# Moebius rounds: products of up to four tiles in one instruction, their sums in another, three buffers

## The reference, cut to what matters

```python
def mobius_add(x, y):
    x2 = jnp.sum(x * x, axis=-1, keepdims=True)
    y2 = jnp.sum(y * y, axis=-1, keepdims=True)
    xy = jnp.sum(x * y, axis=-1, keepdims=True)
    num = (1.0 + 2.0 * xy + y2) * x + (1.0 - x2) * y
    den = 1.0 + 2.0 * xy + x2 * y2
    return num / jnp.maximum(den, EPS)
...
messages = mobius_add(x[src], -x[dst])
def body(out, em):
    m, idx = em
    return (out.at[idx].set(mobius_add(out[idx], m)), None)
total, _ = jax.lax.scan(body, out0, (messages, dst))
```

## Time and profile before

| | |
|---|---|
| median of three runs | 7507.04 us |
| span of the profiled execution, first to last instruction | 7447.1 us |
| busy over the span: PE, DVE, ACT, POOL | 2431.1, 3315.8, 1771.2, 4460.6 us |
| first and last start of a Moebius gather (L1590) | 2729.5 and 4428.6 us |

### The profile page before, as it was taken

One profiled execution on the slowest core, in us unless ns is written; L12 is line 12 of the kernel. 1 busy time (PEld: TensorE's weight loads), 2 busy tenths in 40 slices (PEclk: granted clock), 3 DMA queues, 4 the chain that ended last, 5 costly groups with the idle time before them and its releaser, 6 DMA issues. The chain is left out here.

```text
span 7447.1 us, 57775 instructions
## 1 busy us (share of the span) xinstructions
PE 2431.1 (33%) x12640; PEld 1798.8 (24%) x12640; DVE 3315.8 (45%) x12439; ACT 1771.2 (24%) x5753; POOL 4460.6 (60%) x4570
## 2 busy tenths in 40 slices
PE   5776654666566610000000003555545400000000
PEld 4555544444444410000000002333333200000000
DVE  2333333333343543444444685455555433434466
ACT  1111111111111101222222225666666400000011
POOL 5666664667776655555554435666666657566545
PEclk7677776767787755555555556777777755555555
DMA  4333335665555431111111103333333332122111
GB/s 101 100 99 102 102 98 99 208 185 168 167 166 166 112 87 37 37 37 37 37 37 35 32 18 98 90 95 98 95 93 98 96 84 54 43 51 51 44 33 36
DMA packets 404927, 637.51 MB, mean 86 GB/s; under 512 B 148580, under 2 KB 248966, under 8 KB 404340
## 3 DMA queue, kind: packets, MB, share of 16 engines
q0 software_dynamic: 175664, 424.09, 22.2%
q1 hardware_dynamic: 139076, 115.67, 5.9%
q10 hardware_dynamic: 89856, 94.18, 3.9%
HBM read 529.65 MB, written 103.93 MB: 85 GB/s over the span
## 5 line engine op out<-in xcount | busy, mean ns | idle before, releaser
L1590 POOL DMA_INDIRECT mb_rows<-x_tab,mb_idx x882 | 832.1, 943 | 877.7 <-ACT mb_ps L1638 585.2
L2532 POOL DMA_INDIRECT gt_rows<-h_tab,gt_idx x882 | 847.5, 961 | 497.4 <-issue 269.8
L977 POOL DMA_INDIRECT s_rows<-y_split,srcS x824 | 854.4, 1037 | 418.7 <-issue 226.3
L2035 POOL DMA_INDIRECT eq_ring<-fx_tab,srcS x824 | 816.9, 991 | 441.7 <-issue 235.3
L555 POOL DMA_INDIRECT s_rows<-in_x,srcS x824 | 780.6, 947 | 439.1 <-issue 221.2
L2070 ACT ACTIVATE eq_ring<-eq_ring 128x64 f32<-128x64 f32 x3328 | 860.1, 336 | 442.6 <-issue 332.5
L2111 PE MATMUL eq_ps<-eq_ring,eq_onehot 128*128 128x320 f32 x1664 | 629.3, 538 | 609.8 <-issue 451.0
L1700 PE MATMUL mb_ps<-ident,mb_rows 128*128 128x128 f32 x49 | 12.4, 340 | 1857.5 <-ACT mb_rows L1667 1853.0
L2111 PEld LDWEIGHTS eq_ps<-eq_ring,eq_onehot 128*128 128x128 f32 x1664 | 381.4, 239 | 837.6 <-issue 769.6
L1055 PE MATMUL s_ps<-s_onehot,s_rows 128*128 128x128 bf16 x4992 | 460.1, 253 | 222.6 <-issue 204.7
L194 DVE TENSOR_TENSOR s_onehot<-iota,dstM 128x512 bf16<-128x512 f32 x206 | 142.2, 691 | 743.3 <-PE s_ps L1055 388.3
(11 more groups left out here) (507 smaller groups left out, 5727.7 us busy)
## 6 DMA issues: line engine op xcount, KB each, us to landing
w_tab<-s_wrow ACTq DMA_DIRECT2D x208, 264.0 KB
eq_ring<-w_tab SPq DMA_DIRECT2D x208, 264.0 KB
s_es<-in_side ACTq DMA_DIRECT2D x208, 136.0 KB
mb_rows<-x_tab,mb_idx POOLq DMA_INDIRECT x882
gt_rows<-h_tab,gt_idx POOLq DMA_INDIRECT x882
s_rows<-in_x,srcS POOLq DMA_INDIRECT x824
s_rows<-y_split,srcS POOLq DMA_INDIRECT x824
eq_ring<-fx_tab,srcS POOLq DMA_INDIRECT x824
```

The costliest lines, as they stand in the source:

```text
L977: pool.indirect_dma_start(rows[:, n % SLOTS, :], None, t["ys"], bass.IndirectOffsetOnAxis(ap=s["srcS"][:, n:n + 1], axis=0)).then_inc(gath ...
L1590: pool.indirect_dma_start(rows[:, r, n, :], None, t["x1"], bass.IndirectOffsetOnAxis(ap=idx[:, r, n:n + 1], axis=0)).then_inc(gathered[r][ ...
L2035: pool.indirect_dma_start(frow[:, n % SLOTS, :], None, features, bass.IndirectOffsetOnAxis(ap=s["srcS"][:, n:n + 1], axis=0)).then_inc(gat ...
L2532: pool.indirect_dma_start(rows[:, r, n, :], None, flat, bass.IndirectOffsetOnAxis(ap=idx[:, r, n:n + 1], axis=0)).then_inc(gathered[r][g], 16)
```

## The change

The running products are formed by a chunk. One `tensor_tensor` multiplies the chunk's copied rows, read twice by a broadcast, with own rows and running sums together, up to 2 x 4 x 128 elements; for that, `xd` and `fold` become halves of one tile `xf`. One `tensor_reduce` then sums the products of a chunk into `dots` and `q_`, which become halves of `both`. The sum of chunk c - 1 is issued after the product of chunk c and waits for `multiplied`, which the product now raises. `prod` has three buffers; product c waits until the sum of chunk c - 3 is done. A sync stands before the algebra.

```diff
-        xd = sb("xd", [P, TILES, XW])
+        xf = sb("xf", [P, 2, TILES, XW])
+        xd, fold = xf[:, 0], xf[:, 1, :, 0:D]
         rows = sb("rows", [P, 2, TILES, XW])
-        fold = sb("fold", [P, TILES, D])
...
-        prod = sb("prod", [P, 2, 2, 4, D])
+        prod = sb("prod", [P, 3, 2, 4, D])
         junk = prod[:].rearrange("p a b w d -> p (a b w) d")
-        dots = sb("dots", [P, TILES])
-        q_ = sb("q", [P, TILES])
+        both = sb("both", [P, 2, TILES])
+        dots, q_ = both[:, 0], both[:, 1]
...
                 do = Chain(dve, own)
+                products = lambda c: b * (2 * NC) + (r * NC + (c + 1 if c + 1 < many else NC))
+
+                def add_up(c):
+                    g, lo, hi = CHUNKS[c]
+                    dve.wait_ge(multiplied, products(c))
+                    do.put(dve.tensor_reduce(both[:, :, lo:hi], prod[:, c % 3, :, 0:hi - lo], AX_X, ALU.add))
+
                 for c in range(many):
                     g, lo, hi = CHUNKS[c]
-                    dve.wait_ge(copied_ready, b * (2 * NC) + (r * NC + (c + 1 if c + 1 < many else NC)))
-                    if c >= 2:
-                        do.sync()
-                    for k, other in enumerate((xd, fold)):
-                        for n in range(lo, hi):
-                            ins = dve.tensor_tensor_reduce(out=prod[:, c % 2, k, n - lo], in0=copied(c)[:, n - lo], in1=other[:, n, 0:D],
-                                                           scale=1.0, scalar=0.0, op0=ALU.mult, op1=ALU.add,
-                                                           accum_out=(dots, q_)[k][:, n:n + 1])
-                        if k == 0:
-                            do.put(ins)
-                    ins.then_inc(multiplied, 1 if c + 1 < many else 1 + NC - many)
-                dve.wait_ge(multiplied, b * (2 * NC) + (r * NC + NC))
+                    dve.wait_ge(copied_ready, products(c))
+                    if c >= 3:
+                        dve.wait_ge(own, c - 2)
+                    wide = [P, 2, hi - lo, D]
+                    dve.tensor_tensor(prod[:, c % 3, :, 0:hi - lo], copied(c).unsqueeze(1).broadcast_to(wide), xf[:, :, lo:hi, 0:D],
+                                      ALU.mult).then_inc(multiplied, 1 if c + 1 < many else 1 + NC - many)
+                    if c:
+                        add_up(c - 1)
+                add_up(many - 1)
+                do.sync()
```

## The result

The changed kernel takes 7218.19 us, median of four runs, beside 7508.12 us for the kernel before on the same chip: a ratio of 0.9615, 95% interval [0.9602, 0.9629], or 290 us less. The forecast was 7247 us.

The account below looks back on a forecast made before the run. Moebius gathers wait for VectorE, which a per-instruction throttle from the gathers holds up. Savings 170 + 80 + 20 - 10 = 260 us off the 7447.1 span give 7187, plus 60: 7247 us, range 7170 to 7420.

Parts of the forecast that it names:

- rounds 0 and 1: First Moebius rounds, under a double burst of 98 gathers: products of the second begin as now and end earlier, saving 20 us.
- ten intervals: Burst to burst, Moebius rounds 2 to 12, 49 gathers each: 74.7 instead of 91.7 us, saving 170 us.
- next two, two, four: Later Moebius intervals, shorter bursts: 164.6, 139.8 and 177.6 us become 134.3, 113.8 and 153.6, saving 80 us.
- sixteen small rounds: Moebius rounds of 9, 5 and 1 tiles, hardly held: dearer product, self-wait and sum cost 0.6 us each, 10 lost.
- 3.1 us a chunk: Pace of a chunk's product and sum on VectorE while held by the gathers, taken from GAT's figure.
- what was to show the forecast right: Bursts of 49 some 75 us apart, 2.8 to 3.4 us between full-chunk products, hold over at 68 us, TENSOR_REDUCE near 1.22.
- Algebra in the throttle: VectorE's algebra after the products: 1.4 us per instruction while held, passing 5 or 2 of 30 up to `gm`.
- The median stands 60 above the span: Median 7507 exceeds the profiled span by 60 us, 0.8%, taken as what lies around it, turning 7187 into 7247.
- rival 3: The hold belongs to the profiled execution alone; large timed rounds hide the change, small ones pay: 7525 us, chance 0.05.
- 1, self-waits: VectorE's waits on its own semaphores set the pace, 4.6 us a chunk: 112 us saved, 7395 us, chance 0.14.
- 2, a share of VectorE's time: Gathers withhold VectorE time, not a number of instructions, so extra work costs 135 us: 7642 us, chance 0.11.
- 4, no throttle on products: Products lose the hold altogether, ending at 46 to 51 us, next burst at 72.4: 7210 us, chance 0.10.

## Why the prediction was right, and which terms were off

The mechanism was right: a hold per instruction, which the gathers load and which outlasts them, so that fewer instructions win although their work is dearer. Term by term, saved us in the profiled executions:

| term | predicted | measured | from |
|---|---|---|---|
| rounds 0 and 1 (first gather to burst 2) | 20 | 30.5 | 153.1 to 122.6 |
| ten intervals | 170 | 160.3 | 917.2 to 756.9 |
| next two, two, four | 80 | 95.6 | 164.6, 139.8, 177.6 to 132.3, 111.6, 142.5 |
| sixteen small rounds | -10 | -5.9 | 160.2 to 166.1 |
| sum | 260 | 280.5 | |

- **3.1 us a chunk** was too slow: 15 chunks took 36 to 39 us, 2.4 to 2.6 each. A throttled step took 1.42 us, not GAT's 1.55 (2.80 us between the products of full chunks, the lower end of what was to show the forecast right), of which 1.14 is work for a full chunk, and about the first eight instructions of the round shown went free. In the rounds of 27 tiles all products did (15.5 us a round); that is the largest error within the stretches: 35.1 us saved over the last four intervals, 24 forecast.
- **Algebra in the throttle:** in that odd round 12 of its instructions passed before 3267, not 5. The products ended 57.8 us after the burst began, not 61.4, and the 12 took 9 us, 0.8 each, where 1.4 had been assumed. What that costs and what it gives nearly cancel: once products end inside the throttle, the next burst comes 68.3 us plus the free rest after the last one, whatever the pace, as with the narrow products (73.1 to 73.9). Hence 73 to 75 us an interval (75.7 with the first, 94.8 us, which a double burst precedes), where 74.7 had been forecast, from a chunk pace that was wrong by a fifth.
- **The median stands 60 above the span, "what lies around it":** wrong. In the changed kernel's profiled execution the span is 7216.0 and its own time 7217.74: 1.7 us lie around a span. The profiled execution of before was a quicker one in other stages: its first Moebius gather came at 2729.5 us, the changed kernel's, which changes nothing ahead of it, at 2759.1, and from the last gather to the end it took 3018.5 us against 3039.2. The difference of spans, 231 us, therefore understates the change; the stage's, 280 us, is near the 290 of the medians. The argument against rival 3 rested on the same reading. As priced, at 7525 us, that rival falls, since timed runs gained what the profile gained.
- **Rival 3 in a wider form is open:** the hold could come from the recording of the trace. Every timed run on record has a span and a granted clock of its own, so none is known to have run without recording. Of the 16 increments that each gather makes to its semaphore, the traces record 2.1 on average in the ten intervals before and 1.7 after, but 13.3 and 15.0 in the same two kernels with gathers 1.44 us apart. Where the hold came and went (the changed kernel at 1.40 us), bursts with late folds have 2.2 to 2.9 records a gather and those between them 7.6 to 9.9. So few records and the hold go together; whether recording causes it, no run separates.
- **Rivals.** 1, self-waits: refuted by the run with two buffers and by 2.4 to 2.6 us a chunk. 2, a share of VectorE's time: refuted by half the elements costing the same. 4, no throttle on products: refuted by the 1.42 us steps, though its 7210 us lay nearer to the 7218 measured than the forecast's 7247; its time was near for the reason that intervals hardly depend on the pace. So the time alone doesn't tell rival 4 from the forecast; the steps do.
- **tensor_reduce** (in the trace before also on other lines than the one read, as L2259) is no slower than tensor_tensor here, 994 ns beside 1000 over the same shapes; 1024 elements took 1.22 us, as forecast. What "VectorE: DVE Perf Modes", Rules for kernel authors, of the Trainium skill says of it (VectorE's slowest operation) this kernel doesn't show.

What stays open is what a gather loads. Bytes and rows made no difference, and it isn't the transfer alone, since the hold outlasts it: in the changed kernel

```profile
3261.00:3267.00 6.00, 0.00 (x0) 0.00 (x0) 1.39 (x8) 0.00 (x0) 0.00 (x0) 0.50 0.00 0
3267.20:3271.90 4.70, 0.00 (x0) 0.00 (x0) 4.34 (x25) 1.12 (x4) 0.00 (x0) 0.50 0.00 0
```

no gather is issued and no byte moves (last columns) from 3261 to 3267, yet VectorE gets out 8 instructions in 6 us, and then 25 in 4.7. The packets of a gather, its 16 increments and their records are left as candidates; no run has gathers without a semaphore of their own.

## What to carry to other kernels

When an engine that waits for nothing stands at "issue" while another issues gathers back to back, look at the mean step between starts of short and of long instructions: if it does not follow their length, the hold goes by the instruction. Then either send fewer, longer instructions, or slow the gathers until the hold is gone; the second was worth more here, 4.6% against 3.9%, and left the first nothing to win. Slowing pays only where the paced burst is shorter than the held chain, as GAT's long and short rounds show. All of this was measured with recording on; compare a time without it where you can.

## What was not expected of the hardware

- With gathers at one per 1.25 us VectorE let out one instruction per 1.33 to 1.42 us on average; at 1.44 us products ran unheld in two runs and were held in part in a third, at 1.34 they were held as before, and at 1.40 it came and went: 0.1 us of spacing decides over some 280 us.
- The hold was the same with 264 bytes a row, or with 64 rows a gather.
- A wait for the sum just ahead costs 0.2 us when nothing is held, and nothing that shows in the held rounds.
